# Masking products of half width, and one order of products and masks, in a four-layer graph attention kernel

## The chip, the cores and the metric

One Trainium2 chip; the kernel runs on one of its cores. The metric is the device time of one execution in microseconds (us). Engines are called TensorE (PE in the profile, its weight loads PEld), VectorE (DVE), ScalarE (ACT), GpSimd (POOL) and SyncE (SP).

## The reference, cut to what matters

2048 nodes with 64 features go through four residual blocks: a dense 2048x2048 0/1 adjacency masks a graph attention in each. Blocks 0 and 1 are one attention layer each, block 2 holds two and a small MLP, and block 3 is a softmax attention with a masked matrix and its square. So there are four layers of this kind, and the change concerns those alone:

```python
Wh = h @ W
a1, a2 = (a[:F_OUT, 0], a[F_OUT:, 0])
e = (Wh @ a1)[:, None] + (Wh @ a2)[None, :]
e = jax.nn.leaky_relu(e, negative_slope=ALPHA)
scores = jnp.where(adj > 0, e, jnp.float32(NEG_INF))
attention = jax.nn.softmax(scores, axis=1)
h_prime = attention @ Wh
return jax.nn.elu(h_prime)
```

## The kernel before, in words

Scores are held transposed: source nodes on the 128 partitions, target nodes along the free dimension. The 2048 targets are cut into two chunks of 1024 (`c` = 0, 1), the sources into 16 blocks of 128 (`k`). A layer `l` therefore has 32 tiles of 128 x 1024, and each tile goes round four steps:

- **exponents** (VectorE, line 1284) writes the unmasked score to one of two PSUM tiles `X` of two banks, after ScalarE is through with the tile before the last (`p_ready`).
- **mask** (TensorE, line 758) adds to `X` a very large negative number wherever there is no edge: the stationary operand `bigI` is a 128x128 bf16 identity times 2^100, the moving operand `nadj` is -1 or 0. One product per bank of 512 targets, two in all.
- **exponential** (ScalarE, line 439) reads `X` and writes the tile of probabilities to one of four buffers `prob`.
- **products** (TensorE, line 766) multiplies the tile by `Wh` of its block, fp32, two products of 64 output partitions each: targets 0 to 511 of the chunk into partitions 0 to 63 of the bank `PROD[c]`, targets 512 to 1023 into partitions 64 to 127.

**sums** (TensorE, line 786) adds up the row sums of a pair of tiles in fp32, by four products of 32 output partitions into the bank `S`. For five tiles of each chunk, but the very first, **accumulate** on VectorE (lines 1293 and 1296) does this addition instead, so that two of eight pairs have no sums of their own; `ADD_BEHIND` names the exponents behind which each addition stands in VectorE's order.

Nothing is scheduled: every engine runs the list that the program writes out, in order, and semaphores hold it where it needs another engine. On TensorE that list goes by pairs `p` of tiles `k = 2p` and `k + 1` (lines 875 to 948). The masks run two tiles ahead of the products. Three patterns exist for a pair, P standing for products, M for mask and S for sums: P M P M S in chunk 0 of layers 1 to 3 and in the first four pairs of every chunk 1; P P M M S in layer 0, chunk 0, which has an adjacency product (line 741, `chunk_levels`) behind each S; and P P M M S in pairs 4 to 6 of every chunk 1. The last pair of a chunk 1 has no masks.

Between the pairs of chunk 1 stands what finishes chunk 0 of the same layer: `total` (line 795) and `reciprocal_rows` (804) for the row sums, `centre` (634, 636, 642), `variances` (647) and `features` (666) for the next layer. Each hands over to VectorE and back: VectorE's `reciprocals`, `falling` (1309), `rising` (1312), `clip` (1140), `variance` (1145) and `features` stand among its exponents of chunk 1, and each holds the exponents behind it until TensorE or ScalarE has delivered. Layer 3 has the MLP (812 to 816) there, layer 2 the parameters of layer 3 (697, 701).

Of the kernel before, what the change touches and what calls it, by code (L numbers as in the profile page):

```python
# [9 lines left out]
NB = N // P  # L10
# [4 lines left out]
BANK = 512  # L15
# [31 lines left out]
def program(nc, xT_d, cst_d, late_d, adjT_d, out_d):  # L47
# [4 lines left out]
    with ctx:  # L52
        def sb(name, shape, dt=f32):
            return ctx.enter_context(nc.sbuf_tensor(name, shape, dt))

        def ps(name, shape):
            return ctx.enter_context(nc.psum_tensor(name, shape, f32))
# [4 lines left out]
        nadj = sb("nadj", [P, NB, N], bf16)  # L62
# [34 lines left out]
        bigI = sb("bigI", [P, P], bf16)  # L97
# [66 lines left out]
        X = [ps(f"X{k}", [P, CH]) for k in range(2)]  # L164
# [113 lines left out]
        def added(c_all):  # L278

            if c_all == 0:  # L280
                return ()
            return ((0, 1, 4, 5, 10), (0, 1, 2, 3, 4))[c_all % NCH]
# [48 lines left out]
        def feat(hh):  # L331
            return slice(F * hh, F * (hh + 1))
# [4 lines left out]
        def half_cols(c, hh):  # L337
            return slice(c * CH + hh * BANK, c * CH + (hh + 1) * BANK)
# [267 lines left out]
        def _(pe):  # L606
            pe.wait_ge(consts, N_C)
            pe.wait_ge(ld_c, 16)
            for l in range(2):
                for t in range(2):  # L610
                    pe.matmul(M[0:F, 2 * l + t:2 * l + t + 1], lwT[:, l, t * F:(t + 1) * F],
                              atv[:, l:l + 1], start=True, stop=True)
                last = pe.matmul(M[:, 8 + l:9 + l], lbv[:, l:l + 1].broadcast_to([32, P]), atv[:, l:l + 1],
                                 start=True, stop=True)
            last.then_inc(pe_prep, 1)
            pe.wait_ge(prep_ready, 1)
            for l in range(GAT):
                last = pe.matmul(M[:, 16 + 2 * l:18 + 2 * l], wTt[:, l, :], av[:, l, :], start=True, stop=True)
# [4 lines left out]
            def repeat(bank_of, count):  # L623

                for _ in range(count):
                    pe.matmul(bank_of[:, 0:BANK], bigI[:], nadj[:, 0, 0:BANK], start=True, stop=True)  # L626
# [127 lines left out]
            def mask(l, c, k):  # L754
                t = NB * (NCH * l + c) + k
                pe.wait_ge(x_written, t + 1)
                for hh in range(2):
                    last = pe.matmul(X[t % 2][:, hh * BANK:(hh + 1) * BANK], bigI[:], nadj[:, k, half_cols(c, hh)],  # L758
                                     start=False, stop=True, skip_group_check=True)
                last.then_inc(x_masked, 1)  # L760

            def products(l, c, k):
                t = NB * (NCH * l + c) + k
                pe.wait_ge(p_ready, t + 1)
                for hh in range(2):
                    last = pe.matmul(PROD[c][feat(hh), :], Wh[l % 2][:, k, :], prob[:, t % U, hh * BANK:(hh + 1) * BANK],  # L766
                                     start=k == 0, stop=k == NB - 1)
                if k == NB - 1:
                    last.then_inc(prod_done, 1)
                if k % 2 and k in added(NCH * l + c) and k - 1 in added(NCH * l + c):  # L770
                    last.then_inc(p_free, 1)
# [81 lines left out]
            for n in range(NCH):  # L853
# [3 lines left out]
                      stop=True).then_inc(norm_psum, 1)  # L857
# [6 lines left out]
            for l in range(GAT):  # L864
                top_levels(l)
                if l:
                    w_rows(2 * l + 1)
                repeat(M, 17 if l else 8)
                if l == 0:
                    chunk_levels(1, 0)  # L870
                    chunk_levels(1, 1)
                pe.wait_ge(nv_ready, 4 * (l + 1) if l else 2)
                mask(l, 0, 0)
                mask(l, 0, 1)
                for c in range(NCH):
                    for p in range(NB // 2):
                        k = 2 * p
                        if p == 0 and l == 2:
                            pe.wait_ge(h0_ready, c + 1)
                        if c and p == NB // 2 - 1:  # L880
                            pe.wait_ge(p_ready, NB * (NCH * l + c + 1))
                            sums(l, c, k + 1)
                        if l == 0 and c == 0:
                            products(0, 0, k)
                            products(0, 0, k + 1)
                            if p == 6:
                                shift_products(0, 2, 4)
                            if p < NB // 2 - 1:
                                mask(0, 0, k + 2)
                                mask(0, 0, k + 3)  # L890
                            sums(0, 0, k + 1)
                            for jb in range(4 + k if p else 2, 6 + k if p < 6 else 0):
                                chunk_levels(1, jb)
                            if p == NB // 2 - 1:
                                mask(0, 1, 0)
                                mask(0, 1, 1)
                            continue
                        if c and p >= 4:
                            products(l, c, k)
                            products(l, c, k + 1)  # L900
                            if p < NB // 2 - 1:
                                mask(l, c, k + 2)
                                mask(l, c, k + 3)
                        else:
                            for i in range(2):
                                products(l, c, k + i)
                                if p < NB // 2 - 1:
                                    mask(l, c, k + 2 + i)
                                else:
                                    mask(l, 1, i)  # L910
                        if c == 0 or p < NB // 2 - 1:
                            sums(l, c, k + 1)
                        if c == 0:
                            if p == 0 and l:
                                w_broadcast(2 * l + 1)
                            if p == 2 and l == 2:
                                root_broadcast(1)
                            continue
                        if p == 0:
                            total(l, 0)  # L920
                        if p == 1:
                            reciprocal_rows(l, 0)
                            if l < 2:
                                centre_old(2 * l + 2)
                        if l < 2:
                            if p == 3:
                                centre(2 * l + 2)
                            if p == 4:
                                variances(2 * l + 2)
                        if l < 3:  # L930
                            if p == 2 and l == 2:
                                reach_row()
                            if p == 3 and l == 2:
                                reach_spread()
                            if p == 5:
                                if l == 2:
                                    pe.wait_ge(reachsq_ready, 1)
                                features(2 * l + 2)
                        else:
                            if p == 3:  # L940
                                mlp(0)
                            if p == 4:
                                centre_mlp(0)
                            if p == 5:
                                variances(6)
                                centre_again(0)
                            if p == 6:
                                keys(0)
                total(l, 1)
                if l < 3:  # L950
                    w_rows(2 * l + 2)
                else:
                    repeat(X[0], 2)
                reciprocal_rows(l, 1)
                if l < 2:
                    centre_old(2 * l + 3)
                    early_levels(l + 1, 0, 2)
                    centre(2 * l + 3)
                    w_broadcast(2 * l + 2)
                    variances(2 * l + 3)  # L960
                    early_levels(l + 1, 2, 4)
                    features(2 * l + 3)
                    early_levels(l + 1, 4, CB)
                    repeat(X[0], 2)
                if l == 2:
                    early_levels(l + 1, 0, 3)
                    w_broadcast(2 * l + 2)
                    early_levels(l + 1, 3, CB)
                    features(2 * l + 3)
                    repeat(X[0], 4)  # L970
# [120 lines left out]
            for q in range(1, 4):  # L1091
                for c in range(NCH):
                    n = NCH * q + c
                    for jb in range(NB):
# [8 lines left out]
                        last = propagate(PROD[c] if q % 2 == 0 else X[1][:, c * BANK:(c + 1) * BANK], c, Y[(q + 1) % 2], jb)  # L1103
# [594 lines left out]
```

## Time and profile before

| | us |
|---|---|
| three runs | 614.8, 615.35, 617.01; median 615.35 |
| profiled execution, span from its first to its last instruction | 613.1 |
| what the median has beside that span | 2.2 |
| TensorE matmuls busy | 546.7 (89% of the span) |
| VectorE busy | 394.2 (64%) |
| ScalarE busy | 289.4 (47%) |
| the four attention layers in that span, from the first exponents to the last products | 47.4 to 413 |

The busy time of TensorE counts each matmul from start to a modelled end, and pipelined matmuls overlap; what an operation costs TensorE is read from the start of one group to the start of the next. The profiled execution is one more beside the three timed ones; its own time is known as its span. The mean granted TensorE clock was 0.978 of full speed.

### The profile page before, as it was taken

The page shows a single profiled execution, that of the slowest core. Times are in us where ns is not written, and L with a number is a line of the kernel's source. Part 1 is how long each engine was busy: PE and PEld are TensorE (multiplying, and loading weights), DVE is VectorE, ACT ScalarE, POOL GpSimd, SP SyncE. Part 2 cuts the span into 40 slices and gives each one's busy share as a digit, 9 for nine tenths or more (in the row PEclk, how much of TensorE's full clock was granted, in tenths as well). Part 3 has the DMA queues.
Part 4 walks back from the last instruction along what each step waited for, and adds up shares of the span by engine and source line. Part 5 has one row for each costly group of instructions (what it writes and reads, how often), then busy time and mean ns, then how long its engine had stood idle before and what let it go on. Part 6 is the DMA issues. An engine that isn't in the chain of part 4 may idle for free.

```text
span 613.1 us, 7091 instructions
## 1 busy us (share of the span) xinstructions
PE 546.7 (89%) x2888; PEld 186.5 (30%) x2888; DVE 394.2 (64%) x545; ACT 289.4 (47%) x314; POOL 32.1 (5%) x29
## 2 busy tenths in 40 slices
PE   5687999988999988999888999999887799999997
PEld 3521222333112234212133112245331233433332
DVE  2788879437979446989746988543899987101000
ACT  1387965343655433655433755444767677000000
POOL 0500000201000101000000000021100000000000
PEclk9878999999999999999999999999998889999999
DMA  8867100000000000000000000000000000000000
GB/s 324 297 241 285 57 0 1 1 0 2 1 0 1 0 2 2 1 0 1 0 1 2 0 2 1 0 1 0 2 0 1 0 2 0 1 1 1 1 0 35
DMA packets 5489, 19.39 MB, mean 32 GB/s; under 512 B 592, under 2 KB 592, under 8 KB 5456
## 3 DMA queue, kind: packets, MB, share of 16 engines
q1 hardware_dynamic: 5312, 18.11, 8.2%
q10 hardware_dynamic: 144, 0.82, 0.4%
q8 instruction: 23, 0.38, 0.2%
q14 instruction: 10, 0.08, 0.0%
HBM read 18.40 MB, written 0.52 MB: 31 GB/s over the span
## 4 chain that ended last, share of the span: by engine, by line
PE 61%; DVE 23%; ACT 7%; issue 6%; POOL 1%; DMA 1%; POOLq 0%; DVEq 0%; ACTq 0%
PE PROD L766 13%; PE X L1003 9%; PE X L758 9%; DVE X L1284 7%; PE S L786 7%; PE PROD L1003 6%; DVE aB L1546 6%; ACT big L439 3%; DVE nadj L1563 2%; DVE big L1296 1%; ACT big L485 1%; PE M L626 1%; PE M L721 1%; DMA cst<-in_cst 1%; POOL rr L372 1%
## 5 line engine op out<-in xcount | busy, mean ns | idle before, releaser
L439 ACT ACTIVATE big<-X,v 128x1024 f32<-128x1024 f32 x128 | 140.8, 1113 | 124.3 <-PE X L758 124.2
L1284 DVE SCALAR_TENSOR_TENSOR X<-wB,v,aB 128x1024 f32<-128x1024 f32 x128 | 163.6, 1292 | 24.0 <-ACT big L439 22.4
L766 PE MATMUL PROD<-big,Wh 128*64 128x512 f32 x512 | 134.1, 616 | 1.4 <-ACT big L439 1.3
L758 PE MATMUL X<-nadj,bigI 128*128 128x512 bf16 x256 | 76.7, 386 | 21.7 <-DVE X L1284 21.4
L786 PE MATMUL S<-big,onesf 128*32 128x512 f32 x400 | 53.3, 604 | 3.1 <-DVE big L1296 2.4
L758 PEld LDWEIGHTS X<-nadj,bigI 128*128 128x128 bf16 x256 | 14.9, 97 | 116.3 <-DVE X L1284 80.0
L766 PEld LDWEIGHTS PROD<-big,Wh 128*64 128x64 f32 x512 | 28.0, 136 | 69.1 <-issue 56.3
L1003 PE MATMUL PROD<-big,Wh 128*64 128x512 f32 x128 | 34.0, 654 | 8.3 <-ACT big L554 8.3
L372 POOL TENSOR_TENSOR rr<-var,mhalf 128x8 f32<-128x8 f32 x8 | 16.8, 2163 | 322.5 <-DVE var L1145 322.5
L1003 PE MATMUL PROD<-nadj,Wh 128*64 128x512 f32 x128 | 29.1, 598 | 0.4 <-ACT nadj L554 0.4
L1003 PE MATMUL X<-big,Wh 128*64 128x512 f32 x128 | 28.6, 594 | 0.0
L1003 PE MATMUL X<-nadj,Wh 128*64 128x512 f32 x128 | 28.0, 593 | 0.0
L485 ACT ACTIVATE big<-nadj 128x1024 fp8e4<-128x1024 bf16 x26 | 25.8, 1054 | 3.0 <-DVE nadj L1407 3.0
L1296 DVE TENSOR_TENSOR big<-big 128x1024 f32<-128x1024 f32 x21 | 25.6, 1219 | 0.4
L976 PE MATMUL X<-nadj,bigI 128*128 128x512 bf16 x64 | 19.7, 390 | 2.5 <-ACT big L544 1.4
L554 ACT ACTIVATE big<-big 128x1024 f32<-128x1024 f32 x16 | 16.8, 1057 | 8.8 <-DVE big L1563 8.8
L427 ACT ACTIVATE aB<-X,nvb,nvs 128x512 f32<-128x512 f32 x14 | 9.8, 776 | 23.3 <-PE X L752 23.3
L1563 DVE TENSOR_TENSOR big<-big,aB 128x1024 f32<-128x1024 f32 x16 | 19.4, 1224 | 0.5
L1563 DVE TENSOR_TENSOR nadj<-nadj,aB 128x1024 f32<-128x1024 f32 x16 | 18.4, 1214 | 2.0 <-ACT aB L550 2.0
L979 PE MATMUL X<-wB 96*128 96x512 bf16 x64 | 19.4, 385 | 0.0
L1407 DVE TENSOR_SCALAR nadj<-big 128x1024 bf16<-128x1024 int32 x28 | 19.1, 698 | 0.0
L1546 DVE TENSOR_TENSOR aB<-aB,big 128x1024 f32<-128x1024 f32 x15 | 18.4, 1224 | 0.4
(291 smaller groups left out, 579.5 us busy)
## 6 DMA issues: line engine op xcount, KB each, us to landing
big<-in_adjT SPq DMA_DIRECT2D x28, 512.0 KB, 6.6
aB<-in_adjT SPq DMA_DIRECT2D x4, 512.0 KB, 7.5
cst<-in_cst ACTq DMA_DIRECT2D x1, 800.0 KB, 5.6
x<-in_xT SPq DMA_DIRECT2D x1, 512.0 KB, 6.3
out<-x SPq DMA_DIRECT2D x2, 256.0 KB, 2.0
late<-in_late SPq DMA_DIRECT2D x1, 272.5 KB, 5.3
```

The lines of the kernel that those rows point to most:

```text
L372: pool.tensor_tensor(dst, src, mhalf[:], ALU.pow).then_inc(r_ready, 1)
L439: act.activation(prob[:, t % U, :], X[t % 2][:], ACT.Exp, bias=v2[l % 2][:, k:k + 1]).then_inc(p_ready, 1)
L485: act.activation(adj[:, b, part], nadj[:, b, part], ACT.Identity, bias=1.0, saturate=False).then_inc(adj8_act, 1)
L758: last = pe.matmul(X[t % 2][:, hh * BANK:(hh + 1) * BANK], bigI[:], nadj[:, k, half_cols(c, hh)], start=False, stop=True, skip_group_check ...
L766: last = pe.matmul(PROD[c][feat(hh), :], Wh[l % 2][:, k, :], prob[:, t % U, hh * BANK:(hh + 1) * BANK], start=k == 0, stop=k == NB - 1)
L786: last = pe.matmul(S[32 * strip:32 * strip + 32, :], onesf[:, 0:32], src[:, hh * BANK:(hh + 1) * BANK], start=k == first_sum(c_all), stop= ...
L976: pe.matmul(X[s % 2][:, hh * BANK:(hh + 1) * BANK], bigI[:], nadj[:, jb, half_cols(c, hh)], start=True, stop=False)
L1003: last = pe.matmul(out[feat(hh), :], src[:, jb, :], kept(c, jb)[:, hh * BANK:(hh + 1) * BANK], start=jb == 0, stop=jb == NB - 1)
L1284: dve.scalar_tensor_tensor(X[t % 2][:], wB[:, cols(c)], v8[l % 2][:, k:k + 1], aB[:, cols(c)], ALU.max, ALU.add).then_inc(x_written, 1)
L1296: ins = dve.tensor_tensor(acc[c], acc[c], prob[:, t % U, :], ALU.add)
L1546: ins = dve.tensor_tensor(accf[:, cols(c)], accf[:, cols(c)], kept(c, k), ALU.max)
L1563: dve.tensor_tensor(kept(c, k), kept(c, k), accf[:, cols(c)], ALU.add).then_inc(s_lowered, 1)
```

## The change

Each mask is written by four products in place of two: for each bank, the first 64 columns of `bigI` write partitions 0 to 63 and the other 64 columns write partitions 64 to 127, both from the same 512 moving columns. And the pairs 4 to 6 of every chunk 1 are written in the order of the other pairs, product and mask in turn. Layer 0, chunk 0 keeps its order of two products and then two masks. Nothing moves on another engine.

```diff
@@ mask
                 for hh in range(2):
-                    last = pe.matmul(X[t % 2][:, hh * BANK:(hh + 1) * BANK], bigI[:], nadj[:, k, half_cols(c, hh)],
-                                     start=False, stop=True, skip_group_check=True)
+                    for side in range(2):
+                        last = pe.matmul(X[t % 2][feat(side), hh * BANK:(hh + 1) * BANK], bigI[:, feat(side)],
+                                         nadj[:, k, half_cols(c, hh)], start=False, stop=True, skip_group_check=True)
                 last.then_inc(x_masked, 1)
@@ the loop over pairs
-                        if c and p >= 4:
-                            products(l, c, k)
-                            products(l, c, k + 1)
+                        for i in range(2):
+                            products(l, c, k + i)
                             if p < NB // 2 - 1:
-                                mask(l, c, k + 2)
-                                mask(l, c, k + 3)
-                        else:
-                            for i in range(2):
-                                products(l, c, k + i)
-                                if p < NB // 2 - 1:
-                                    mask(l, c, k + 2 + i)
-                                else:
-                                    mask(l, 1, i)
+                                mask(l, c, k + 2 + i)
+                            elif c == 0:
+                                mask(l, 1, i)
```

`feat(side)` is the slice of 64 columns or partitions. In the changed file the lines of `mask`, `products` and `sums` are 759, 767 and 787.

TensorE, layer 1, chunk 0, one pair with its sums, before (a row's size is output partitions by columns, then how many matmuls):

```order
L766 MATMUL PROD0<-big,Wh1 64x512 x2
L758 MATMUL X0<-nadj,bigI 128x512 x2
L766 MATMUL PROD0<-big,Wh1 64x512 x2
L758 MATMUL X1<-nadj,bigI 128x512 x2
L786 MATMUL S<-big,onesf 32x512 x4
```

and the same pair in the changed kernel:

```order
L767 MATMUL PROD0<-big,Wh1 64x512 x2
L759 MATMUL X0<-nadj,bigI 64x512 x4
L767 MATMUL PROD0<-big,Wh1 64x512 x2
L759 MATMUL X1<-nadj,bigI 64x512 x4
L787 MATMUL S<-big,onesf 32x512 x4
```

The order is the same; the masks now have the output height of the products beside them, and twice their number.

TensorE, layer 1, chunk 1, from the centring for layer 2 (lines 634, 636) over pair 4 to the variances (647) and pair 5, before:

```order
L634 MATMUL PROD0<-big,cst 128x512
L636 MATMUL PROD0<-big,cst 128x512
L766 MATMUL PROD1<-big,Wh1 64x512 x4
L758 MATMUL X0<-nadj,bigI 128x512 x2
L758 MATMUL X1<-nadj,bigI 128x512 x2
L786 MATMUL S<-big,onesf 32x512 x4
L647 MATMUL M<-cst,sq 128x2 x4
L766 MATMUL PROD1<-big,Wh1 64x512 x4
L758 MATMUL X0<-nadj,bigI 128x512 x2
```

and in the changed kernel:

```order
L634 MATMUL PROD0<-big,cst 128x512
L636 MATMUL PROD0<-big,cst 128x512
L767 MATMUL PROD1<-big,Wh1 64x512 x2
L759 MATMUL X0<-nadj,bigI 64x512 x4
L767 MATMUL PROD1<-big,Wh1 64x512 x2
L759 MATMUL X1<-nadj,bigI 64x512 x4
L787 MATMUL S<-big,onesf 32x512 x4
L647 MATMUL M<-cst,sq 128x2 x4
L767 MATMUL PROD1<-big,Wh1 64x512 x2
L759 MATMUL X0<-nadj,bigI 64x512 x4
```

Here the mask of the first tile moves ahead of the second tile's products, and the second products now stand between the two masks.

## Rows read from the trace of the kernel before

**Rows 1.** Busy time by stretch: layer 0 chunk 0, layer 1 chunks 0, 1, layer 2 chunk 1. Each row: stretch, length, then the engines.

```profile
core 0: us, PE busy (x) PEld busy (x) DVE busy (x) ACT busy (x) POOL busy (x), PEclk, DMA share, GB/s
47.40:87.50 40.10, 36.80 (x192) 9.09 (x192) 32.13 (x35) 29.73 (x30) 0.00 (x0) 0.96 0.33 116
...
150.04:181.17 31.13, 29.57 (x136) 5.67 (x135) 27.45 (x25) 18.79 (x18) 0.00 (x0) 1.00 0.00 1
181.17:223.90 42.73, 39.46 (x204) 11.48 (x202) 28.90 (x38) 20.31 (x21) 2.62 (x1) 1.00 0.00 1
...
277.38:320.00 42.62, 36.36 (x195) 10.15 (x194) 31.33 (x49) 20.02 (x21) 0.93 (x1) 1.00 0.00 1
```

**Rows 2.** Groups of instructions: exponents and masks, busy us, mean ns, idle before them, releaser.

```profile
L1284 DVE SCALAR_TENSOR_TENSOR X<-wB,v,aB 128x1024 f32<-128x1024 f32 x128 | 163.6, 1292 | 24.0 <-ACT big L439 22.4
...
L758 PE MATMUL X<-nadj,bigI 128*128 128x512 bf16 x256 | 76.7, 386 | 21.7 <-DVE X L1284 21.4
```

**Rows 3.** Timeline of TensorE, layer 1 chunk 0: start us, length us, group.

```profile
172.99 0.61 PE L758 MATMUL X<-nadj,bigI 128*128 128x512 bf16 x2
173.52 1.08 PE L766 MATMUL PROD<-big,Wh 128*64 128x512 f32 x4
174.53 0.60 PE L758 MATMUL X<-nadj,bigI 128*128 128x512 bf16 x2
175.07 1.06 PE L786 MATMUL S<-big,onesf 128*32 128x512 f32 x8
176.06 1.08 PE L766 MATMUL PROD<-big,Wh 128*64 128x512 f32 x4
177.07 0.61 PE L758 MATMUL X<-nadj,bigI 128*128 128x512 bf16 x2
```

**Rows 4.** The same view, layer 3 chunk 1, pair 6.

```profile
404.33 1.94 PE L766 MATMUL PROD<-big,Wh 128*64 128x512 f32 x8
406.20 1.04 PE L758 MATMUL X<-nadj,bigI 128*128 128x512 bf16 x4
407.17 1.06 PE L786 MATMUL S<-big,onesf 128*32 128x512 f32 x8
```

**Rows 5.** The same view, layer 0 chunk 0: sums, adjacency product, products.

```profile
64.46 1.07 PE L786 MATMUL S<-big,onesf 128*32 128x512 f32 x8
65.36 0.60 PE L741 MATMUL M<-big,level 128*32 128x512 fp8e4 x4
65.89 1.94 PE L766 MATMUL PROD<-big,Wh 128*64 128x512 f32 x8
```

**Rows 6.** Instructions of line 766, then 786, in rows 4 and 5: duration ns min/median/max.

```profile
L766 PEld LDWEIGHTS PROD<-big,Wh x8: 132/136/137, 404.3 to 405.2; 128*64 128x64 f32 x8
L766 PE MATMUL PROD<-big,Wh x8: 592/592/643, 404.3 to 405.7; 128*64 128x512 f32 x8
...
L786 PEld LDWEIGHTS S<-big,onesf x8: 106/108/110, 64.5 to 64.5; 128*32 128x32 f32 x8
```

**Rows 7.** Timeline of all engines, layer 1 chunk 0: exponents and mask of tile 9.

```profile
165.01 1.28 DVE L1284 SCALAR_TENSOR_TENSOR X<-wB,v,aB 128x1024 f32<-128x1024 f32 x1
...
166.35 0.60 PE L758 MATMUL X<-nadj,bigI 128*128 128x512 bf16 x2 [0.71 <-DVE X L1284]
```

**Rows 8.** Timeline of VectorE, layer 1: exponents of tile 13, then of chunk 1.

```profile
173.09 1.28 DVE L1284 SCALAR_TENSOR_TENSOR X<-wB,v,aB 128x1024 f32<-128x1024 f32 x1
...
187.04 1.29 DVE L1284 SCALAR_TENSOR_TENSOR X<-wB,v,aB 128x1024 f32<-128x1024 f32 x1
...
189.79 2.55 DVE L1296 TENSOR_TENSOR big<-big 128x1024 f32<-128x1024 f32 x2
...
192.96 1.29 DVE L1284 SCALAR_TENSOR_TENSOR X<-wB,v,aB 128x1024 f32<-128x1024 f32 x1
```

**Rows 9.** Timeline of all engines, layer 1 chunk 1: clip, masks of tiles 11 and 13.

```profile
205.18 0.69 DVE L1140 TENSOR_SCALAR g<-PROD 128x512 f32<-128x512 f32 x1 [2.58 <-ACT sq L411]
...
207.25 0.60 PE L758 MATMUL X<-nadj,bigI 128*128 128x512 bf16 x2 [0.34 <-DVE X L1284]
...
212.50 0.61 PE L758 MATMUL X<-nadj,bigI 128*128 128x512 bf16 x2 [0.25 <-DVE X L1284]
```

## The prediction

> **What bounds the kernel now.** I first read the busy time by stretch [rows 1]. In the chunks of layers 1 to 3 TensorE is busy nearly throughout (29.6 of 31.1 us in layer 1, chunk 0), but VectorE is close behind (27.5 of 31.1), and in chunk 1 of layer 2 TensorE is idle for over 6 of 42.6 us. So the second view matters as much: before masks TensorE sits idle for 21.7 us in total, nearly all of it until VectorE has written the exponents [rows 2]. Two regimes alternate: TensorE sets the pace, or a ring exponents, mask, exponential, exponents does, with VectorE's additions and hand-overs in it. Only the first can gain from cheaper TensorE work.
>
> The third view, TensorE's timeline, gives prices, from the start of one group to the start of the next [rows 3]. A steady pair P M P M S takes 177.07 - 172.99 = 4.08 us: masks 0.53 and 0.54, sums 0.99, products 1.01 each. Two products in a row take 1.87 [rows 4], so products that are followed by products cost 0.86, and leaving them for a mask costs 0.15. Two masks in a row take 0.97 [rows 4]: a mask followed by a mask costs 0.43, leaving one 0.11. Part of this is weight loading that shows after a changeover: the first product matmul of a group has 643 ns against 592, 0.05 us [rows 6].
>
> **The change, part by part.** *What the changeover hangs on.* Products have 64 output columns, masks 128, sums 32. Sums followed by the adjacency product, of 32 columns too but another data type, take 65.36 - 64.46 = 0.90 us, 0.09 less than sums followed by products [rows 3, 5]. So where the width stays, the changeover goes, even from fp32 to a product with bf16 weights. I take it that products and 64-column masks behave the same.
>
> *The mask of four products.* The trace of before has none. From below, it costs what a mask costs without a changeover, 0.43; from above, if its two halves did not run side by side, 0.86. The nearest row is the adjacency product: four narrow matmuls of 512 columns with different weights, two at a time, take 65.89 - 65.36 = 0.53 with the changeover behind them [rows 5], just what a mask takes now. I take 0.43 within the same width and 0.54 ahead of sums.
>
> *A pair.* P M P M S becomes 0.91 (0.05 of loading stays behind the sums) + 0.43 + 0.86 + 0.54 + 0.99 = 3.73, against 4.08: 0.35 saved, as 0.10 (first products), 0.11 (mask), 0.15 (second products). P P M M S is 1.87 + 0.97 + 0.99 = 3.83 today, so there only 0.10 is left to save. If TensorE set the pace everywhere, a chunk 0 of layers 1 to 3 would save about 3.0 (six pairs with sums at 0.35, two without at 0.4 to 0.5), a chunk 1 1.85 (four pairs at 0.35 to 0.45, three at 0.10), layer 0 2.5: 17 us in all. That is the ceiling, and the waits take most of it.
>
> *A load with a wait.* Where a mask waits for exponents, its first weights are loaded after the wait. A load of 64 columns takes 26 to 28 ns more than one of 32 [rows 6], and I charge as much, an estimate, to each such mask on the path, about 7 in a layer: 28 x 0.027 = 0.75 us. The Trainium skill (TensorEngine Tiling, Restrictions and Gotchas) says that column tiling excludes Fast Weight Load, which speaks against the change; no run here shows a 64-column bf16 load.
>
> Here the skill has a stronger rule against it, too (TensorE: Matmul & The Clock Gate, Part 3): weight loads overlap matmuls in flight only if their row groups differ, and here all use all 128 rows. The trace disagrees: two products in a row, every matmul with a load of 132 to 137 ns, take 4 x 0.43 and no more [rows 4, 6]. By the rule each mask would pay for its loads, which is the third rival below, worked out from rows.
>
> *Layer 1, chunk 0 (31.1 us).* Up to tile 9 the ring sets the pace: exponents, an addition of some 1.3 us (half of 2.55) [rows 8], exponents, and mask 9 starts at 166.35 after 0.71 us of waiting [rows 7]. Only mask 6, ahead in that ring, comes earlier for TensorE's sake: 0.4 us. From 166.35 on TensorE runs without a gap for 14.8 us, three pairs and a half, worth 3 x 0.35 + 0.10 = 1.15. But mask 13, at 174.53 [rows 3], has exponents that end at 173.09 + 1.28 = 174.37 behind an addition [rows 8]; they move only as their ring does, and hold it for 0.45 us of that gain. Sum 0.4 + 1.15 - 0.45 = 1.1.
>
> *Layer 1, chunk 1 (42.7 us).* Exponents at 187.04, then two additions that take 2.55 us from 189.79, then `falling`, then exponents at 192.96 [rows 8]. `falling` waits for `reciprocal_rows` on TensorE, which comes 1.0 us earlier, but the additions, in front of it, only 0.3. From the sums of pair 2 to the centring TensorE is the path again: 0.10 + 0.11 + 0.15 = 0.36. After that, centring, square, clip (205.18), exponents, mask 11 (207.25), variances, exponents, mask 13 (212.50), features hand over in turn [rows 9]; TensorE's groups between them are single, and nothing more is gained.
>
> *The new order.* Mask of tile k + 2 moves ahead of products k + 1. Queued behind its wait are now these products, the next mask and the sums. In pair 4 mask 10 has its exponents early and mask 11 still waits for the clip: no effect. In pair 5 mask 12 starts earlier but products 11 now end 0.09 us after the time at which mask 13 could go: a loss of 0.09. In pair 6 the second products run while mask 15 waits for its exponents anyway: nothing. No DMA, and no other engine's list, moves.
>
> *Sum.* Layer 1: 1.1 + 0.3 + 0.36 - 0.09 = 1.7. Layer 3: the same, with TensorE without a gap in pair 6 [rows 4], 0.1 more and no loss in pair 5: 1.9. Layer 2, with twice layer 1's idle TensorE in chunk 1 [rows 1]: 0.7, an estimate. Layer 0: chunk 0 keeps P P M M, and half of its six times 0.10 is lost to exponents; chunk 1 saves the 0.36: 0.65. Together 4.95, less 0.75 for loads: 4.2 us. The span of 613.1 becomes 608.9; the median of the runs lies 2.2 above the span, 615.35, and becomes **611.1**. The stages after the attention layers are untouched and shift with them.
>
> **The rivals.** *The waits eat more.* VectorE's list is only 3.7 us shorter than layer 1, chunk 0 [rows 1]; if the ring rather than TensorE decides in the gapless stretch too, half the gain is left: 613.2. For it: 21.4 us of waiting on VectorE today. Against it: before mask 12 to 15 TensorE shows no gap. 16%.
>
> *Changeovers stay.* What costs time might be going from fp32 products to bf16 masks rather than the width. Then nothing is saved, and the three pairs P P M M S of each chunk 1 get two changeovers more, of which one a layer lies on the path, 0.25 each: 616.3. Against it rows 5; for it, that no row has 64 columns in bf16. 8%.
>
> *The mask gets longer, and the kernel slower.* Place: every mask. If its four loads are not hidden, at twice the 0.13 of a load [rows 6], a mask costs 0.26 more. About 19 masks a layer lie on the path, waiting ones too, since their length is part of the ring; some 80 in all: + 20.8 - 4.2, 632. It decides early: at 80 masks, 0.05 us more per mask undoes the gain, and 0.09 makes the kernel slower by over 0.5%. Halves one after the other (0.43 more) would give 645. Against it the adjacency product [rows 5]. 8%.
>
> *TensorE is the path more often than I count.* Ceiling 17 us, 598; likelier some 7 to 9 us, 607. 8%.
>
> **How the numbers follow.** The forecast has 60%, its own range being 609 to 613 (loads at nothing or at twice the charge, mask 13 waiting or not, layers 0 and 2 at half or double). The three runs shown spread over 2.2 us, 0.36%; about 0.5%, 3.1 us, can be told from no change, so faster means below 612.3. Nine tenths of the forecast and the last rival are faster: 0.62. The rest of the forecast, the first rival and most of the second make no difference: 0.29. Slower: the third and a little of the second, 0.09. The range leaves out the third rival, the far half of the second and the ceiling: 606.5 to 615.5.
>
> **What would show it.** In the profile after: a pair P M P M S in layer 1, chunk 0 at 3.7 us in place of 4.08, products to mask at 0.86, sums still 0.99; mask 13 with a gap before it that waits for VectorE; more idle time before masks in total than 21.7 us, by some 10 us, since what TensorE saves mostly turns into waiting; chunk 0 of layers 1 and 3 at 30 us, chunk 1 of layer 1 at 42.1. A pair at 4.08 or above would show the second rival, masks above 0.5 us the third. I am wrong if TensorE saves 0.35 a pair and the attention layers shrink by less than 2 us or by more than 8.

## The result and the profile after

The changed kernel takes **607.37 us** (median of 4 runs, 605.64 to 609.0) against 615.08 (4 runs, 614.64 to 617.01) of the kernel before, run alternately: ratio **0.9861**, 95% interval 0.983 to 0.9892. By the ratio that is 8.5 us, by the medians 7.7. The forecast was 4.2 us, a time of 611.1; the direction and the wide range (606.5 to 615.5) hold, the forecast's own 609 to 613 does not, and the size is half of what came. The profiled span went from 613.1 to 604.9 us.

The page of the changed kernel: span, busy time of the engines, the groups of exponents (L1278), products (L767) and masks (L759) with their weight loads, and the summary of the chain of waits.

```profile
span 604.9 us, 7603 instructions
...
PE 533.1 (88%) x3144; PEld 197.7 (33%) x3144; DVE 393.1 (65%) x545; ACT 290.3 (48%) x314; POOL 31.8 (5%) x29
...
PE 53%; DVE 29%; ACT 8%; issue 6%; POOL 1%; DMA 1%; POOLq 0%; DVEq 0%; ACTq 0%
...
L1278 DVE SCALAR_TENSOR_TENSOR X<-wB,v,aB 128x1024 f32<-128x1024 f32 x128 | 163.4, 1292 | 19.2 <-ACT big L439 17.8
L767 PE MATMUL PROD<-big,Wh 128*64 128x512 f32 x512 | 135.1, 612 | 1.5 <-ACT big L439 1.3
L759 PE MATMUL X<-nadj,bigI 128*64 128x512 bf16 x512 | 79.1, 389 | 27.0 <-DVE X L1278 26.3
L759 PEld LDWEIGHTS X<-nadj,bigI 128*64 128x64 bf16 x512 | 24.7, 110 | 113.5 <-DVE X L1278 86.8
```

Twice as many mask matmuls occupy TensorE for 79.1 us where 256 wide ones took 76.7 [rows 2]: the halves run side by side. TensorE waits longer for exponents (27.0 us for 21.7), and VectorE's share of the chain rose from 23% to 29%. VectorE's idle time before exponents, nearly all of it for ScalarE, fell from 24.0 to 19.2 us.

The pair behind that of [rows 3] in the timeline of TensorE (products 12 and 13, masks 14 and 15), with the mask of tile 13 and its sums ahead of it (start us, length us, group, idle before it and releaser):

```profile
170.99 0.62 PE L759 MATMUL X<-nadj,bigI 128*64 128x512 bf16 x4 [0.35 <-DVE X L1278]
171.54 1.07 PE L787 MATMUL S<-big,onesf 128*32 128x512 f32 x8
172.54 1.08 PE L767 MATMUL PROD<-big,Wh 128*64 128x512 f32 x4
173.44 0.60 PE L759 MATMUL X<-nadj,bigI 128*64 128x512 bf16 x4
173.88 1.03 PE L767 MATMUL PROD<-big,Wh 128*64 128x512 f32 x4
174.74 0.60 PE L759 MATMUL X<-nadj,bigI 128*64 128x512 bf16 x4
175.27 1.07 PE L787 MATMUL S<-big,onesf 128*32 128x512 f32 x8
176.26 1.08 PE L767 MATMUL PROD<-big,Wh 128*64 128x512 f32 x4
```

From the products of tile 12 to those of tile 14 it takes 176.26 - 172.54 = **3.72 us** in place of 4.08. The starts give 0.90 for the products behind the sums, 0.44 for a mask, 0.86 for the second products, 0.53 for the mask ahead of the sums, 0.99 for these: each within 0.01 of the forecast.

By stretch, as in [rows 1] (layer 0 chunk 0; layer 1 chunks 0 and 1; layer 2 chunk 1; PEclk is the granted TensorE clock as a share of full speed). Layer 1's stretches run from the first mask of a chunk:

```profile
core 0: us, PE busy (x) PEld busy (x) DVE busy (x) ACT busy (x) POOL busy (x), PEclk, DMA share, GB/s
44.22:84.75 40.53, 37.49 (x224) 10.53 (x224) 32.17 (x35) 29.73 (x30) 0.00 (x0) 0.92 0.37 128
...
147.09:177.17 30.08, 27.73 (x167) 7.57 (x168) 27.32 (x25) 18.79 (x18) 0.00 (x0) 1.00 0.00 1
177.17:219.00 41.83, 38.00 (x237) 13.19 (x233) 28.82 (x38) 20.52 (x21) 2.63 (x1) 1.00 0.00 1
...
271.36:313.90 42.54, 35.22 (x227) 11.41 (x223) 31.37 (x49) 20.11 (x21) 0.93 (x1) 1.00 0.00 0
```

In layer 1, chunk 0, TensorE works 27.73 us for 29.57 and the chunk takes 30.08 for 31.13. In chunk 1 of layer 2 over a microsecond less work gives 0.08: there the time goes into waiting. Layer 0, chunk 0, is 0.43 longer, with a granted clock of 0.92 for 0.96. Layer 0 therefore can't be judged from this execution alone, nor can the place of the first exponents: 44.22 here, 47.38 before, in front of anything that the change touches. The attention layers, from the first exponents to the start of the last product matmul of layer 3, went from 365.03 to 359.88 us, 5.2 less; the other 3 us of the span lie ahead of them.

### The profile page after: what moved, and what is told of

Read it like the earlier page. It is cut to its first block, busy times and chain, and to the rows that moved or that the text cites. A ratio compares the mean times of both kernels' runs of the same rounds, so it can differ in the third digit from the quotient of the medians.

```text
span 604.9 us, 7603 instructions
## 1 busy us (share of the span) xinstructions
PE 533.1 (88%) x3144; PEld 197.7 (33%) x3144; DVE 393.1 (65%) x545; ACT 290.3 (48%) x314; POOL 31.8 (5%) x29
## 4 chain that ended last, share of the span: by engine, by line
PE 53%; DVE 29%; ACT 8%; issue 6%; POOL 1%; DMA 1%; POOLq 0%; DVEq 0%; ACTq 0%
DVE X L1278 11%; PE X L997 9%; PE PROD L767 9%; PE X L759 7%; PE PROD L997 7%; PE S L787 6%; DVE aB L1540 6%; ACT big L439 5%; DVE big L1290 2%; DVE nadj L1557 2%; ACT big L485 1%; PE M L626 1%; PE M L721 1%; DVE big L1287 1%; DMA cst<-in_cst 1%
## 5 line engine op out<-in xcount | busy, mean ns | idle before, releaser
L1278 DVE SCALAR_TENSOR_TENSOR X<-wB,v,aB 128x1024 f32<-128x1024 f32 x128 | 163.4, 1292 | 19.2 <-ACT big L439 17.8
L767 PE MATMUL PROD<-big,Wh 128*64 128x512 f32 x512 | 135.1, 612 | 1.5 <-ACT big L439 1.3
L759 PE MATMUL X<-nadj,bigI 128*64 128x512 bf16 x512 | 79.1, 389 | 27.0 <-DVE X L1278 26.3
L759 PEld LDWEIGHTS X<-nadj,bigI 128*64 128x64 bf16 x512 | 24.7, 110 | 113.5 <-DVE X L1278 86.8
L767 PEld LDWEIGHTS PROD<-big,Wh 128*64 128x64 f32 x512 | 31.8, 137 | 53.9 <-issue 30.4
L970 PE MATMUL X<-nadj,bigI 128*128 128x512 bf16 x64 | 19.7, 390 | 2.5 <-ACT big L544 1.4
```

What stands on the lines that cost most here:

```text
L759: last = pe.matmul(X[t % 2][feat(side), hh * BANK:(hh + 1) * BANK], bigI[:, feat(side)], nadj[:, k, half_cols(c, hh)], start=False, stop=T ...
L970: pe.matmul(X[s % 2][:, hh * BANK:(hh + 1) * BANK], bigI[:], nadj[:, jb, half_cols(c, hh)], start=True, stop=False)
L1278: dve.scalar_tensor_tensor(X[t % 2][:], wB[:, cols(c)], v8[l % 2][:, k:k + 1], aB[:, cols(c)], ALU.max, ALU.add).then_inc(x_written, 1)
```

## Experiments

Two theories stood. **A**: the gain is the cheaper changeovers in the attention layers, 5 to 6 us; the rest belongs to single executions, of whichever kernel. **B**: the change also gives 2 to 3 us outside those layers, by the clock that the start gets.

**The two kernels again, unaltered.**

```diff
 (no edit)
```

> The changed kernel unaltered. Theory A (the four attention layers save 5.2 us, and the further 3.2 us by which the first exponents came earlier in its profile are the clock that TensorE happens to be granted in the start stage, which the change does not touch): over many rounds the saving is 5 to 6 us, ratio 0.990 to 0.992, and the first exponents of this profile may stand anywhere between 44 and 48 us; from first exponents to last products of layer 3 it takes 360.5 us as in the first profile of the changed kernel. Theory B (the earlier start belongs to the change): ratio 0.986 again, and first exponents at 44 us again.

> The kernel of before unaltered. Theory A: ratio 1.000, first exponents anywhere between 44 and 48 us, and 365.5 us from there to the last products of layer 3. Theory B: first exponents at 47 us again.

Measured: 606.08 us for the changed kernel (5 runs, 605.29 to 608.95), ratio 0.9853 (0.9827 to 0.9879); 616.46 for the one before (12 runs), ratio 1.0008 (0.9992 to 1.0025). The profiles have the attention layers at 359.27 and 365.04 us, 5.8 apart as A said, and the first exponents at 47.17 and 49.25, the second past the 48 that A allowed. By stretch (start, attention layers, rest), first the kernel before in the execution that the forecast was made from:

```profile
0.00:47.38 47.38, 30.26 (x128) 17.10 (x128) 29.79 (x74) 21.22 (x25) 9.54 (x16) 0.86 0.81 291
47.38:412.40 365.02, 336.26 (x1884) 100.97 (x1886) 266.09 (x341) 190.71 (x202) 17.93 (x11) 1.00 0.04 13
412.40:613.10 200.70, 180.17 (x878) 68.44 (x874) 98.30 (x130) 77.51 (x87) 4.62 (x3) 0.97 0.01 3
```

and the changed kernel in its second profile:

```profile
0.00:47.17 47.17, 29.02 (x127) 16.77 (x128) 29.82 (x75) 21.22 (x25) 9.54 (x16) 0.89 0.78 288
47.17:406.44 359.27, 323.98 (x2136) 114.36 (x2142) 265.23 (x341) 191.56 (x202) 17.95 (x11) 1.00 0.04 14
406.44:607.10 200.66, 179.51 (x873) 68.43 (x874) 98.30 (x130) 77.52 (x87) 4.61 (x3) 0.97 0.01 3
```

With equal starts and equal rests the attention layers differ by 5.75 us, and the spans by 6.0. Yet by the ratio the timed runs differ by 9 us. The change in the layers is settled by this; A as stated, a ratio of 0.990 to 0.992, is not what the runs gave. From here the two places are looked at apart.

**The mask alone, and the order alone.**

The first kernel is the one before with this edit; the second is the changed kernel with this edit undone, so that the new order meets the wide mask.

```diff
-last = pe.matmul(X[t % 2][:, hh * BANK:(hh + 1) * BANK], bigI[:], nadj[:, k, half_cols(c, hh)],
+for side in range(2):
+    last = pe.matmul(X[t % 2][feat(side), hh * BANK:(hh + 1) * BANK], bigI[:, feat(side)],
+                     nadj[:, k, half_cols(c, hh)],
...
```

> Masks by four products, pairs 4 to 6 of the second chunks left at two products and then two masks. If the width of the output is what the changeover hangs on: within 0.5 us of the changed kernel, since in those pairs only 0.10 us of 3.83 was left to save and masks there mostly wait for VectorE; pairs P M P M S at 3.72 us. If the new order carried part of the gain: 1 us or more behind the changed kernel.

> The new order with masks of two products. Theory width: two more changeovers in each of three pairs of a second chunk, of which about one pair a layer lies on the path, 0.25 us each: 0.5 to 1.5 us slower than the kernel before, ratio 1.001 to 1.0025; pairs P M P M S at 4.08 us. If the order itself helped: faster than before by 1 us or more.

Measured: the mask alone 608.52 us (4 runs, 605.36 to 608.76), ratio 0.9866 (0.984 to 0.9891), attention layers 359.06 us. The order alone 616.27 (12 runs), ratio 1.001 (0.9987 to 1.0033), attention layers 366.62, 1.6 longer than before. As far as the runs can tell, the mask makes the whole gain. Of the 1.6 us, 1.3 lie in the second chunks, where the order changed (63.27, 65.34, 60.54 and 45.72 us for 62.88, 64.96, 60.50 and 45.22, from exponents to exponents, the last to the start of the last products); the other 0.3 lie in layer 0, chunk 0, which has the old order. So the new order with wide masks costs in the profile about what its expectation put on extra changeovers, though the timed runs don't tell it from nothing; with narrow masks it gives nothing that shows (359.06 without it, 359.27 with it).

**Width, or number of matmuls.** Two other ways to cut a mask: into four matmuls with all 128 columns and half as many targets, and into eight with 32 columns. The first in the kernel before:

```diff
-for hh in range(2):
-    last = pe.matmul(X[t % 2][:, hh * BANK:(hh + 1) * BANK], bigI[:], nadj[:, k, half_cols(c, hh)],
+for part in range(4):
+    at = part * (BANK // 2)
+    last = pe.matmul(X[t % 2][:, at:at + BANK // 2], bigI[:], nadj[:, k, c * CH + at:c * CH + at + BANK // 2],
...
```

and the second in the changed kernel:

```diff
-for side in range(2):
-    last = pe.matmul(X[t % 2][feat(side), hh * BANK:(hh + 1) * BANK], bigI[:, feat(side)],
-                     nadj[:, k, half_cols(c, hh)],
+for strip in range(4):
+    rows = slice(32 * strip, 32 * strip + 32)
+    last = pe.matmul(X[t % 2][rows, hh * BANK:(hh + 1) * BANK], bigI[:, rows],
+                     nadj[:, k, half_cols(c, hh)],
...
```

> The kernel before with every mask written by four products too, but of 128 output columns and 256 targets each: the number of TensorE instructions of the changed kernel with the old width. Theory width: the changeovers stay, a pair P M P M S takes 4.1 us or a little more, the attention layers take 365 to 367 us as before. If the number of products were what helped: 3.72 us a pair. For the part outside the attention layers, where the changed kernel is also some 3 us faster: if that comes with the longer TensorE program (more instructions, nothing else in common), this kernel has it too and is 2 to 3 us faster than before; if it does not, the ratio is 1.000 to 1.003.

> The changed kernel with every mask written by eight products of 32 output columns. If equal width is what saves the changeover: masks now change over from and to the products of 64 and go without it ahead of the sums of 32, so a pair has four changeovers in place of two and takes 3.97 us (3.72 and two more of 0.10 to 0.15), the attention layers 362.5 to 365 us in place of 359.3. If any narrow output will do: 3.72 us a pair and 359.3. If more and narrower products cost time of their own: masks above 0.5 us, over 366.

The pair of [rows 3] in the timeline of TensorE, with 32 columns (products 10 to 12, masks 12 and 13, and the products of tile 14):

```profile
171.93 1.08 PE L768 MATMUL PROD<-big,Wh 128*64 128x512 f32 x4
172.94 0.61 PE L760 MATMUL X<-nadj,bigI 128*32 128x512 bf16 x8
173.48 1.08 PE L768 MATMUL PROD<-big,Wh 128*64 128x512 f32 x4
174.54 0.62 PE L760 MATMUL X<-nadj,bigI 128*32 128x512 bf16 x8
174.98 1.03 PE L788 MATMUL S<-big,onesf 128*32 128x512 f32 x8
175.94 1.08 PE L768 MATMUL PROD<-big,Wh 128*64 128x512 f32 x4
...
179.91 0.65 PE L768 MATMUL PROD<-big,Wh 128*64 128x512 f32 x2
```

Here products to mask cost 1.01 again and the mask 0.54, but the mask ahead of the sums, which have its width, 0.44: the changeover has moved to another edge. The pair takes 4.01, with some 0.05 us in which mask 13 waits for its exponents (they end at 174.48); the next, from 175.94 to 179.91, takes the 3.97 that was expected. The attention layers take 364.15, the run 611.30 us (10 runs, 610.55 to 616.57), ratio 0.9939 (0.991 to 0.9967). With 128 columns and 256 targets a pair takes 4.10, the layers 365.78, the run 614.83 (10 runs), ratio 0.9993 (0.9971 to 1.0015). So it is the **equal column count of neighbours** that saves, not the number of matmuls, and not the element type, which still changes from f32 to bf16 at every edge.

**VectorE's additions one step later.** Mask 13 waits for exponents that stand behind an addition, and so does mask 9. Three of the four additions of each first chunk go one tile later (`ADD_BEHIND`, the entry of the first chunks), in the changed kernel and in the one before.

```diff
-{3: (1,), 6: (4,), 8: (5,), 12: (10,)}
+{3: (1,), 7: (4,), 9: (5,), 13: (10,)}
```

> The changed kernel with three of VectorE's four additions in the first chunks of layers 1 to 3 moved one exponents later (behind tiles 7, 9 and 13 in place of 6, 8 and 12). If VectorE's additions hold masks 7, 9 and 13 now that TensorE needs 3.72 us a pair: masks 9 and 13 no longer wait, each of these chunks is 0.5 to 1.2 us shorter than 29.6 us, 1.5 to 3.5 us in all. If TensorE sets the pace there: nothing.

> The kernel before with the same three additions moved. With TensorE at 4.08 us a pair, mask 9 is still the only one that waited (0.71 us): up to 0.7 us a layer, 1 to 2 us in all; if the additions were the pace all along, as much as in the changed kernel, 1.5 to 3.5.

In the changed kernel masks 9 and 13 no longer wait. In the timeline of TensorE, mask 9 without the edit:

```profile
163.00 0.62 PE L759 MATMUL X<-nadj,bigI 128*64 128x512 bf16 x4 [0.75 <-DVE X L1278]
```

and with it the first mask of the chunk, masks 9 and 10, products 11 and mask 13:

```profile
149.46 0.62 PE L759 MATMUL X<-nadj,bigI 128*64 128x512 bf16 x4
...
164.34 0.60 PE L759 MATMUL X<-nadj,bigI 128*64 128x512 bf16 x4
...
167.37 0.62 PE L759 MATMUL X<-nadj,bigI 128*64 128x512 bf16 x4 [0.43 <-DVE X L1278]
...
171.55 1.03 PE L767 MATMUL PROD<-big,Wh 128*64 128x512 f32 x4
172.40 0.60 PE L759 MATMUL X<-nadj,bigI 128*64 128x512 bf16 x4
```

The first chunks of layers 1 and 3 take 28.67 us from exponents to exponents (29.57 without the edit), the attention layers 356.7, 2.6 less; the run 604.28 (6 runs, 604.15 to 605.87), ratio 0.9818 (0.979 to 0.9847). The gain lies ahead of mask 9, not at mask 13: from the chunk's first mask to mask 9 it takes 164.34 - 149.46 = 14.88 us, without the edit 163.00 - 147.09 = 15.91, and from there on nothing is gained, since mask 10 now waits 0.43. The same edit in the kernel before brings the chunks of layers 1 and 3 0.26 each and layer 2's 0.39, 0.9 us in all, and a run of 613.43 (10 runs), ratio 0.9967 (0.9943 to 0.9991). By the profiled chunks it is worth about three times as much once TensorE is cheaper: part of what the changed kernel saves on TensorE was held by VectorE's order. The timed runs don't show the difference: by the ratios the edit brings 2.0 us in the kernel before and 2.2 to 2.6 in the changed one.

**The start made the same.** If the start stage decides the other 2 to 3 us, 25 further products of `c16`, which change no output, ahead of and between the start's own matmuls should bring the first exponents to one time in both kernels. The edit is made in the kernel before, the changed one and the one with later additions.

```diff
+def warm(count):
+    for _ in range(count):
+        pe.matmul(X[0][:, 0:P], c16[:], c16[:], start=True, stop=True)
...
+warm(12)
 pe.wait_ge(ld_c, 16)
...
+warm(3 if n else 5)
 w_rows(n)
+warm(3 if n else 2)
 w_broadcast(n)
```

> The kernel before with 25 products of constants put into TensorE's waits of the start stage (12 ahead of the first load's arrival, 13 around the row transposes), which write a bank that is cleared later. If the clock that TensorE is granted in the start stage is what moves the first exponents between 44 and 49 us from one execution to the next: first exponents at 42 to 45 us, 3 us or more faster than the kernel before, and less spread between runs (5 us before).

> The changed kernel with the same 25 products. Theory A (the change is worth what the attention layers save, 5.8 us, and the rest is the clock of the start stage): with both warmed, this kernel is 5 to 7 us faster than warm_before, and first exponents stand within 1 us of those of warm_before. Theory B (the change itself also saves 3 us outside the layers): 8 to 10 us faster than warm_before.

> The changed kernel with the additions of the first chunks one exponents later, and the same 25 products: the version that should beat both kernels. Attention layers at 356.7 us as without the products, 2.6 us less than warm_after in all; ratio to the kernel before 0.977 to 0.981.

First exponents in the timeline of VectorE, warmed, kernel before:

```profile
43.23 1.29 DVE L1291 SCALAR_TENSOR_TENSOR X<-wB,v,aB 128x1024 f32<-128x1024 f32 x1
```

and changed:

```profile
43.21 1.29 DVE L1285 SCALAR_TENSOR_TENSOR X<-wB,v,aB 128x1024 f32<-128x1024 f32 x1
```

The last products of layer 3 in the timeline of TensorE, kernel before:

```profile
407.87 1.94 PE L771 MATMUL PROD<-big,Wh 128*64 128x512 f32 x8
```

and changed:

```profile
402.06 1.94 PE L772 MATMUL PROD<-big,Wh 128*64 128x512 f32 x8
```

Both start at 43.2, and from the exponents to the start of the products lie 364.64 and 358.85 us: 5.79 apart (365.99 and 360.19 to the last of their matmuls, where the attention layers end in the other sections). The runs: 613.25 (12 runs, 612.44 to 615.29) and 606.91 (5 runs, 606.25 to 608.76), **6.3 us** apart, within A's 5 to 7. Of the expectation of 3 us or more for the kernel before only 1.7 came (ratio 0.9972, 0.9958 to 0.9986): the start is 4 us earlier than in its first profile, but the attention layers take 365.99 us and the rest 202.06, 1.0 and 1.3 longer. The runs spread about as much as unwarmed ones of the same rounds, 2.9 us for 3.1. The changed kernel gains nothing by warming (ratio 0.987, 0.9848 to 0.9892). With later additions 603.62 (6 runs, 602.94 to 607.83), ratio 0.9821 (0.9792 to 0.9851): the lowest median of the study, but not told apart from 604.28 without warming, and short of the 0.977 to 0.981 expected; its first exponents came at 43.95 and its layers took 357.5 us.

## Why the forecast was right in kind and half in size

**Right: the mechanism and its prices.** Five prices of a pair came within 0.01 us, so did the pair, 3.72 for 3.73. Width and not type makes a changeover, as read from [rows 5]; the run with 32 columns shows the edge move with the width. In these runs a changeover costs about 0.1 us on a mask (0.44 and 0.53) and 0.15 on products (0.86 and 1.01). The Trainium skill (TensorEngine Tiling (Array Packing), Key Properties) says that a switch of tiling mode requires a drain. The runs agree, if a change of the column count is such a switch. The second and third rivals fell: no changeover stayed between products and masks, and no mask in a gapless stretch got longer. The first fell too, since the layers gave 5.8 us and not half of 4.2. The last, TensorE the path more often than counted, has the measured time (7 to 9 us, 607) but only part of the cause: the layers gave less than its 7.

**Nearly right: the price of a load.** The 64-column bf16 load, which no row of before had, takes 110 ns, against 97 for the wide one. This is in line with the rule that column tiling excludes Fast Weight Load (the Trainium skill, TensorEngine Tiling (Array Packing), Restrictions and Gotchas). Hidden behind matmuls the load costs nothing that shows; the first mask matmul behind a wait has 403 ns, for 379 without one and for 389 behind a wait in the kernel before: 0.014 to 0.024 us more, where 0.027 was charged. The Trainium skill's other rule (TensorE: Matmul & The Clock Gate, Part 3), that loads overlap only across row groups, would have made each mask longer. Masks of four loads that take 0.44 us disagree.

**Right: mask 13.** It waits 0.35 us for exponents behind an addition, and layer 1, chunk 0, took 30.08 us (forecast 30.0), chunk 1 41.83 (42.1).

**Wrong, the step that failed:** the sum puts everything outside the layers at nothing. It says "The stages after the attention layers are untouched and shift with them", which held (200.7 to 200.8 us in the first profile of the kernel before and in both of the changed one), but the stages ahead of the layers are not in the sum at all, without a reason. The base was not off: 611.1 is in effect the median of three runs, 615.35, less 4.2, and the result has 615.08. But 8.5 us came (6.6 to 10.5 by the interval) and 5.8 of them in the layers, so some 2.7 lie where no instruction changed. In ten unwarmed profiles the first exponents came at 45.76 to 49.25 us with wide masks (five profiles) and at 44.22 to 47.41 with narrow ones (five). The nine runs of the changed kernel lie in two groups, 605.3 to 606.7 (five) and 608.0 to 609.0 (four); its first profile is from the first group and reaches chunk 1 of layer 0 at 82.97 us, its second is from the other and reaches it at 85.32. None of the five wide profiles is there before 85.5, and none of 85 runs of the kernel before is below 613.7. With the start warmed alike both kernels are there at 82.5 and 82.3, and 6.3 us are left, of which 5.8 are the layers'. So the extra goes with what an execution does up to that point, though by their intervals 8.5 and 6.3 are not told apart for certain. Why the changed kernel's runs get the early start so much more often is **not settled**. It is not the number of matmuls: the version with 256 targets has as many as the changed kernel and no such gain. Nor does every run with narrow masks have it: the mask alone gave 605.36 with its first exponents at 44.90, and 608.4 to 608.76 in its other three runs.

**Mis-sized: the sum in the layers**, 4.2 for 5.8, from exponents to exponents (layer 3 to its last products) in the undisturbed second profile:

| layer | forecast, us | measured, us |
|---|---|---|
| 0 | 0.65 | 38.35 - 38.15 + 62.88 - 62.70 = 0.38 |
| 1 | 1.7 | 30.26 - 29.57 + 64.96 - 63.66 = 1.99 |
| 2 | 0.7 | 31.26 - 30.52 + 60.50 - 60.07 = 1.17 |
| 3 | 1.9 | 30.26 - 29.57 + 46.56 - 45.03 = 2.22 |
| loads | -0.75 | in the layers above |

The table counts from exponents, so part of what TensorE saves in a chunk 0 falls to chunk 1; from mask to mask chunk 0 of layer 1 came as summed, 1.05 for 1.1. Three terms make the gap. In chunk 1 of layers 1 and 3 the additions were to come "only 0.3" earlier. The exponents behind them and `falling` (tile 6), in the timeline of VectorE of the changed kernel:

```profile
188.24 1.28 DVE L1278 SCALAR_TENSOR_TENSOR X<-wB,v,aB 128x1024 f32<-128x1024 f32 x1
```

They start 188.24 - 177.17 = 11.07 us after the chunk's first mask, and 192.96 - 181.17 = 11.79 before [rows 1, 8]: 0.7 in place of 0.3. Layer 2's 0.7, an estimate from the idle TensorE of its chunk 1, missed its chunk 0, which behaves like layer 1's and alone gives 0.74. And the 0.75 for loads does not show as a cost of that size beside these: one load comes to 0.014 to 0.024, and how many such masks lie on the path is not shown.

**Wrong: the idle time.** It was to rise "by some 10 us, since what TensorE saves mostly turns into waiting". It rose by 5.3, to 27.0. TensorE's 12.3 us less work in the layers (336.26 to 323.98) became 5.75 us of time, nearly half. The ring itself did not get shorter where its mask waits. Tile 9 of layer 1, chunk 0, in the timeline of all engines, the exponential before [its exponents in rows 7]:

```profile
167.00 1.12 ACT L439 ACTIVATE big<-X,v 128x1024 f32<-128x1024 f32 x1 [1.21 <-PE X L758]
```

and exponents and exponential after:

```profile
161.65 1.29 DVE L1278 SCALAR_TENSOR_TENSOR X<-wB,v,aB 128x1024 f32<-128x1024 f32 x1
...
163.66 1.11 ACT L439 ACTIVATE big<-X,v 128x1024 f32<-128x1024 f32 x1 [1.22 <-PE X L759]
```

From the end of the exponents to the exponential 0.71 us before, 0.72 after.

**The new order:** the loss of 0.09 in pair 5 of layer 1 is there in the timeline of TensorE of the changed kernel: mask 12, products, mask 13, without a gap before mask 13, whose exponents end at 207.37.

```profile
206.23 0.62 PE L759 MATMUL X<-nadj,bigI 128*64 128x512 bf16 x4 [0.45 <-DVE X L1278]
206.68 1.02 PE L767 MATMUL PROD<-big,Wh 128*64 128x512 f32 x4
207.54 0.60 PE L759 MATMUL X<-nadj,bigI 128*64 128x512 bf16 x4
```

Mask 13 goes at 207.54, about 0.1 us later than its exponents would allow. Without the new order the second chunks of layers 0 and 1 take 62.58 and 63.56 us for 62.70 and 63.66, those of layers 2 and 3 the same as with it: that is the whole 0.2 us between 359.06 and 359.27, a loss that the timed runs can't show.

## What to carry to other kernels

Where matmul groups alternate on TensorE, give neighbours the same number of output columns, even at the price of more matmuls: here it saved 0.36 of 4.08 us a pair, and the element type did not matter. Then look again at the engine that waits less now: moving three additions on VectorE shortened the profiled layers by 0.9 us before the change and by 2.6 after it. And ask, before a sum puts a stage that the change does not touch at nothing, how much that stage varies between executions.

## What the runs showed of the hardware

The start stage runs the same matmuls at different speeds from one execution to the next. The eight matmuls of line 647, before and then after, in the timeline of TensorE:

```profile
15.24 1.87 PE L647 MATMUL M<-cst,sq 128*128 128x2 f32 x8 [0.32 <-ACT sq L411]
```

```profile
15.21 1.05 PE L647 MATMUL M<-cst,sq 128*128 128x2 f32 x8 [0.47 <-ACT sq L411]
```

1.87 and 1.05 us for the same work at the same time after the same predecessors. The granted clock goes with it. In the trace of the kernel before its record has its first entry at 22.66 us, in the changed kernel's at 14.46, both at full speed, 2.4 GHz; for a stretch ahead of the first entry the views print 1.00, which is no reading. In seven of the ten unwarmed profiles the first entry stands at 22.66 us or later and these matmuls take 1.87; in the other three, of kernels with wide and with narrow masks, it stands at 14.15 to 14.46 and they take 1.05. The first exponents follow: 46.88 to 49.25 us in the seven, 44.22 to 45.76 in the three. Warmed, the first entry comes at 6.82 to 7.95 us. What the engine had ahead of its first entry is not recorded; 1.87 for 1.05 points to the lower of its two levels, 1.2 GHz.

What such an early start gains is not all kept. Warmed, the kernel before lost 2.3 of its 4.2 us in the layers and the rest, where the clock of a stretch was lower instead: 0.91 for 0.96 in layer 0, chunk 0, and 0.96 for 0.97 behind the layers. The changed kernel's first profile, with its first exponents at 44.22, has the 0.92 in layer 0. And the kernel before with later additions had its first exponents at 45.76, but took 39.95 us for 38.35 in layer 0, chunk 0, and began chunk 1 at 85.71 as in its first profile (85.73).
